# Centred rows, fp16 latents and a residual in the accumulator banks in a three-stage transformer layer

## The reference

```
x = x + xattn(layernorm(x), ctx[4096 x 512], mask)    # 16 heads of 32, output bias, layer norm of the scaled result
x = x + latent_attention(layernorm(x))                # 16 heads, causal
x = x + experts(layernorm(x))                         # top 8 of 48 kept experts, capacity 192
```

```
cq    = rms_norm(h @ w_qa.T, q_a_ln_w)                # 384 latents for each token
q     = cq @ w_qb.T                                   # for each head 128 plain and 64 rotary channels
ckv   = h @ w_kva.T                                   # 128 latents and 64 rotary key channels, the latter shared by all heads
k_pe  = k_pe * cos + rotate_half(k_pe) * sin
kv    = rms_norm(ckv[..., :128], kv_a_ln_w) @ w_kvb.T
out   = softmax(q k^T * scale, causal) v, @ w_o.T
```

## Time and profile before

| | us |
|---|---|
| median of 3 runs | 749.24 (747.83 to 749.28) |
| the profiled execution | 750.56 |
| its span, first to last instruction | 748.7 |
| TensorE busy | 719.0 |
| VectorE, ScalarE, GpSimd busy | 610.7, 428.7, 10.3 |

### The profile page before, as it was taken

One profiled execution on the slowest core, in us unless ns is written; L12 is line 12 of the kernel. 1 busy time (PEld: TensorE's weight loads), 2 busy tenths in 40 slices (PEclk: granted clock), 3 DMA queues, 4 the chain that ended last, 5 costly groups with the idle time before them and its releaser, 6 DMA issues.

```text
span 748.7 us, 16362 instructions
## 1 busy us (share of the span) xinstructions
PE 719.0 (96%) x6667; PEld 446.3 (60%) x6667; DVE 610.7 (82%) x940; ACT 428.7 (57%) x585; POOL 10.3 (1%) x30
## 2 busy tenths in 40 slices
PE   7999999999999999897999988999999999999997
PEld 3644444444444444455777757677777777777774
DVE  4578999999999988687788965788888888888885
ACT  3677777777777786623568733444444444444441
POOL 2000000000000000010000000000000000000000
PEclk9999999999999999999999999999999999999999
DMA  8920101010100100031242500497777777777760
GB/s 318 330 67 1 58 2 57 3 58 7 52 3 1 43 17 2 3 133 82 75 135 87 193 36 1 137 285 236 241 223 236 239 232 244 218 241 237 243 208 29
DMA packets 29576, 93.78 MB, mean 125 GB/s; under 512 B 5920, under 2 KB 15056, under 8 KB 28112
## 3 DMA queue, kind: packets, MB, share of 16 engines
q1 hardware_dynamic: 29232, 92.97, 37.8%
q10 hardware_dynamic: 288, 0.02, 0.0%
HBM read 92.37 MB, written 0.57 MB: 124 GB/s over the span
## 4 chain that ended last, share of the span: by engine, by line
PE 85%; DVE 6%; issue 4%; ACT 3%; POOL 1%; POOLq 0%; DVEq 0%; ACTq 0%
PE pS L1134 39%; PE pP L1134 26%; PE pO L1134 10%; PE pD L1134 8%; DVE x_sb L827 2%; ACT arena L508 2%; PE pO L1462 1%; DVE arena L714 0%; DVE bn L863 0%; DVE arena L842 0%; DVE arena L962 0%; DVE arena L914 0%; DVE xn L708 0%; ACT arena L558 0%; DVE work L868 0%
## 5 line engine op out<-in xcount | busy, mean ns | idle before, releaser
L1134 PE MATMUL pS<-arena 128*128 128x256 f16 (+2 forms) x2128 | 252.6, 275 | 5.1 <-DVE arena L962 1.3
L1134 PE MATMUL pP<-arena 128*128 128x512 f16 x968 | 236.4, 383 | 7.0 <-DVE arena L714 7.0
L1134 PEld LDWEIGHTS pS<-arena 128*128 128x128 f16 (+2 forms) x2128 | 212.0, 101 | 50.0 <-ACT arena L575 2.2
L1134 PEld LDWEIGHTS pP<-arena 128*128 128x128 f16 x968 | 90.9, 99 | 131.6 <-issue 11.7
L508 ACT ACTIVATE arena<-pS,mblk 128x1024 f32<-128x1024 f32 x128 | 147.3, 1205 | 11.5 <-PE pS L1134 11.5
L962 DVE SCALAR_TENSOR_TENSOR arena<-arena 128x1536 f16<-128x1536 f32 x72 | 126.0, 1752 | 0.6 <-ACT arena L613 0.5
L651 ACT ACTIVATE arena<-pS 128x256 f32<-128x256 f32 x72 | 27.6, 383 | 155.9 <-PE pS L1134 155.9
L815 DVE TENSOR_SCALAR arena<-arena 128x1024 f32<-128x1024 f32 x128 | 87.2, 690 | 26.2 <-ACT arena L508 23.1
L613 ACT ACTIVATE arena<-arena 128x1536 f16<-128x1536 f32 x72 | 106.3, 1477 | 1.0 <-DMA arena<-in_units 1.0
L1134 PE MATMUL pO<-arena 128*32 128x256 f32 (+6 forms) x1358 | 104.4, 359 | 2.4 <-DVE arena L952 1.9
L1134 PE MATMUL pD<-arena 128*128 128x512 f16 x288 | 76.5, 379 | 1.0 <-DVE arena L1106 1.0
(11 more groups left out here) (242 smaller groups left out, 504.7 us busy)
## 6 DMA issues: line engine op xcount, KB each, us to landing
arena<-in_units SPq DMA_DIRECT2D x72, 768.0 KB, 4.7
arena<-w_scratch SPq DMA_DIRECT2D x136, 64.0 KB, 2.7
arena<-in_ctxT SPq DMA_DIRECT2D x7, 1024.0 KB, 5.1
mw_in<-in_mla_in SPq DMA_DIRECT2D x8, 832.0 KB, 6.7
mw_out<-in_mla_out SPq DMA_DIRECT2D x8, 512.0 KB, 3.7
wlatT<-in_wlatT SPq DMA_DIRECT2D x1, 1280.0 KB, 11.4
arena<-in_wkT SPq DMA_DIRECT2D x4, 256.0 KB, 4.4
arena<-in_ctxT SPq DMA_DIRECT2D x4, 256.0 KB, 6.3
```

The source lines that it names most:

```text
L1134: return pe.matmul(o, lhsT, rhs, start=start, stop=stop, **kw)
```

## The change

1. Output bias of the cross-attention: ScalarE and VectorE make two fp16 halves of it, in rows 0 and 32 of `bo16`, and `out_rows` starts each bank with a product of `onerow` and `bo16`. VectorE takes statistics and centres straight from the bank.
2. Rows: VectorE's last step of `x1_sb` also gives the row sum; `xn` is `x1_sb` less its mean. Column sums, `center`, `scale_kpe` go. The variance comes from a square with row sum on ScalarE.
3. Latents: the weights are split in the last context block (`wlh`, `wll`); transposed rows are split too (`xh`, `xl`); products in fp16 in three parts. The latents' norm weights come as a row and are applied while scaling.
4. Keys are rotated in token rows (`rotate_keys`, table `cs_r`) ahead of their transposition, then split.
5. Latents are transposed and split by tile; the first head pair is projected by token halves (`first_proj`).
6. `prep_experts` moves into the last head pair. The cast of its output weights moves ahead of the exps on ScalarE. Unit 3 is split by ScalarE at the end of the last pair, by VectorE ahead of the copy of `wT`.
7. Residual: `residual(t)` adds `x1_sb`, times 4096, to `pD` and `pP` with an fp32 product in the last pair. Statistics and `xn` are taken from the banks, which stay open through the experts; both `add_zero` there go.
8. `lo_x(1)` goes ahead of `top_of(0)`; `gate_up(1)` is done in two halves around the transposition of the weights; in the last turn `gate_up(71)` goes ahead of `down(69)`. The two output tiles are scaled out by VectorE and ScalarE and stored by a DMA each.

```diff
+                    if last and i < HC:
+                        if i == 0:
+                            act.wait_ge(s["const_ready"], 1)
+                            act.wait_ge(s["row_in"], 64)
+                            act.activation(bo16[0:1, :], bo_b[0:1, :], ACT.Copy, scale=SW)
+                            act.activation(bo_t[32:33, :], bo_b[32:33, :], ACT.Copy, scale=SW).then_inc(s["bo_hi"], 1)
+                            act.wait_ge(s["lat_in"], 16)
+                        act.activation(wlh[:, i], wlatT[:, i], ACT.Copy, scale=SW).then_inc(s["wl_hi"], 1)
...
-                link(dve.tensor_tensor(work[:, t, :], d_ps[t], bo_b[:, :], ALU.add))
-                half_stats(work, t)
+                link(dve.bn_stats(bn[:, t, :], d_ps[t]))
+                link(dve.bn_aggr(mv[:, t, :], bn[:, t, :]))
...
+                link(dve.scalar_tensor_tensor(x1_sb[:, t, :], work[:, t, :], rstd[:, t:t + 1], x_sb[:, t, :],
+                                              ALU.mult, ALU.add, accum_out=xsum[:, t:t + 1]))
+                link(dve.tensor_scalar(xmean[:, t:t + 1], xsum[:, t:t + 1], 1.0 / HID, None, ALU.mult))
+                dve.tensor_scalar(xn[:, t, :], x1_sb[:, t, :], xmean[:, t:t + 1], None, ALU.subtract).then_inc(s["xn_ready"], 1)
...
-            rope_k_products()
-            lo_latents()
-            rope_k()
-            lo_k(0, 0, 1)
-            rope_mul(0, 0, 3)
+            lo_rows(0)
+            row_vars(0)
+            lo_rows(1)
+            rotate_keys(0)
+            row_vars(1)
+            add_eps(0)
+            norm_latents(0)
+            rotate_keys(1)
+            add_eps(1)
+            lo_latents(0)
+            norm_latents(1)
+            dve.wait_ge(s["kpe_hi"], 1)
+            dve.scalar_tensor_tensor(kpel, kpeT, SH / (SX * SW), kpeh, ALU.mult, ALU.subtract).then_inc(s["kpe_ready"], 1)
+            lo_latents(1)
...
+            def latents(t, low):
+                if low:
+                    pe.wait_ge(s["xl1_ready"], t + 1)
+                else:
+                    pe.wait_ge(s["xT_ready"], t + 2)
+                for o, lo, hi, done in ((kpe_ps[t], LAT, LAT + 2 * DR, "kpe_mm"), (lat_raw[t], 0, LAT, "lat_mm")):
+                    for c in range(HC):
+                        for x, w in (((xl, wlh),) if low else ((xh, wlh), (xh, wll))):
+                            last = mm(o, x[:, c, 128 * t:128 * t + 128], w[:, c, lo:hi], not low and c == 0 and w is wlh,
+                                      low and c == HC - 1)
+                    if low:
+                        last.then_inc(s[done], 1)
...
+            first_proj(0)
+            turn_latents(1)
+            first_proj(1)
             pe.wait_ge(s["kpe_ready"], 1)
             add_zero((pD[:, :], pP[:, :]), True, False)
             mla_pair(0, 0, before=False)
...
                 mla_scores(m, p, apart=True)
                 out_product(m - 1, 1 - p, 0)
+                residual(0)
                 turned(0)
+                residual(1)
                 weighted(0)
...
             lo_x(0)
+            lo_x(1)
             top_of(0)
             choose(0)
-            lo_x(1)
...
             last.then_inc(s["w_ready"], 1)
+            split_unit(AHEAD, AHEAD)
             dve.wait_ge(s["wt_done"], 1)
             dve.tensor_copy(wT, wt_ps).then_inc(s["wt_ready"], 1)
...
-                    if not (last_turn and u + 1 >= UNROLL) and not (first and u < 2):
+                    if not (last_turn and u + 2 >= UNROLL) and not (first and u < 2):
                         gate_up(n + 1, (u + 1) % 3, (u + 1) % RING)
-                    down(n, u % RING, u % 3)
+                    if last_turn and u + 3 == UNROLL:
+                        gate_up(n + 2, (u + 2) % 3, (u + 2) % RING)
+                    down(n, u % RING, u % 3, last_turn and u + 1 == UNROLL)
```

More of the change, by code:

```diff
@@ L33 @@
 SA, SW, SH = 64.0, 256.0, 16.0
+SX = 16.0
 NEG = -1.0e30
@@ L233, in build @@
         wnew = take(T)
+        lnw_b = take(LAT)
+        cs_r = take(TT * 2 * DR).rearrange("p (t i d) -> p t i d", t=TT, i=2)
+        bo16, bo_t = (take(HID, f16) for _ in range(2))
+        onerow = sb("onerow", [128, 128], f16)
         assert x_end <= ARENA
@@ L836, in x_block @@
                         (prep_scales, prep_rows)[i]()
+                    if last and i in (2, 3):
+                        for c in (2 * i - 4, 2 * i - 3):
+                            dve.wait_ge(s["wl_hi"], c + 1)
+                            dve.scalar_tensor_tensor(wll[:, c], wlatT[:, c], SW, wlh[:, c], ALU.mult, ALU.subtract)\
+                               .then_inc(s["wl_lo"], 1)
                     if last and i in (4, 6):
@@ L907, in add_eps @@
+                link(last)
+                for i, op in ((0, ALU.subtract), (1, ALU.add)):
+                    last = dve.tensor_tensor(kpn[:, t, i], kcos[:, t, i].unsqueeze(1).broadcast_to([128, 2, DR]),
+                                             ksin[:, t, 1 - i].unsqueeze(1).broadcast_to([128, 2, DR]), op)
+                last.then_inc(s["kpn_ready"], 1)
             def add_eps(t):
@@ L1372, in proj_q @@
+            def proj_q(m):
+                pe.wait_ge(s["qkv_ready"], 3 * m)
+                pe.wait_ge(s["qk_lo"], 2 * m)
+                pe.wait_ge(s["rope_ready"], m)
                 pe.wait_ge(s["mq_lo"], m + 1)
-                for r in ((1, 0) if first else (0, 1)):
-                    if r and not first and not (isinstance(m, int) and m == 1):
+                for r in range(2):
+                    if r and not (isinstance(m, int) and m == 1):
                         pe.wait_ge(s["a_lo"], m - 1)
@@ L1526, in _, with gate_up @@
                 last.then_inc(s["logits_done"], 1)
-            add_zero((pD[:, :], pP[:, :]), True, False).then_inc(s["down_done"], 1)
-            def gate_up(n, bank, ring):
+            def gate_up(n, bank, ring, halves=(0, 1)):
                 pe.wait_ge(s["unit_lo"], n + 1)
-                for half in range(2):
+                for half in halves:
                     k = 0
@@ L1539, in gate_up, with down @@
                             k += 1
-                last.then_inc(s["gu_done"], 1)
-            def down(n, ring, buf):
+                if 1 in halves:
+                    last.then_inc(s["gu_done"], 1)
+            def down(n, ring, buf, end=False):
                 pe.wait_ge(s["h_lo"], n + 1)
                 for t, o in enumerate((pD, pP)):
-                    for h, w in ((hh, uwh), (hh, uwl), (hl, uwh)):
-                        last = mm(o[:, :], h[:, buf, 128 * t:128 * t + 128], w[:, ring, HC * 256:UW], False, False,
+                    for k, (h, w) in enumerate(((hh, uwh), (hh, uwl), (hl, uwh))):
+                        last = mm(o[:, :], h[:, buf, 128 * t:128 * t + 128], w[:, ring, HC * 256:UW], False, end and k == 2,
                                   skip_group_check=True)
-                last.then_inc(s["down_done"], 1)
+                    if end:
+                        last.then_inc(s["moe_done"], 1)
+                if not end:
+                    last.then_inc(s["down_done"], 1)
             pe.wait_ge(s["xl_ready"], TT)
```

304 lines of the change are left out of this document (156 added, 148 removed).

## The result

The changed kernel takes 737.83 us, the median of 4 runs (737.12 to 738.79); the kernel before took 749.26 beside it (747.83 to 749.96). The ratio is 0.985, with a 95% interval of 0.983 to 0.987: 11.4 us faster. The profiled execution took 737.29 us, span 735.6, against 750.56 and 748.7 before, so the spans differ by 13.1 us.

The account below looks back on a forecast made before the run. TensorE, busy 719.0 of 748.7 us, was taken as the bound, with gains only in three seams where it waits. Terms summed to -12.85 us, giving 737.7 (profiled) or 736.4 (median); forecast 737.0, range 734.3 to 741.2.

Parts of the forecast that it names:

- Part 1: Last context block, ahead of the first seam: added ScalarE casts cost 0.6 us, two output-bias products 0.4; together +1.0 us.
- Part 2: First seam, first output product to first latent-attention scores: 23.0 us instead of 26.9, so -3.9 us.
- Rival (b): First seam doesn't shorten: thirteen hand-overs each 0.3 us late use up the 3.9 us; total 740.3 us, chance 0.17.
- Part 3: First scores of the latent attention: 36 score matmuls at full clock take 2.20 us instead of 3.37; -1.1 us.
- Part 4: Last head pair and way into the experts: fourth unit starts at 465.0 instead of 471.1 us; -6.1 us.
- Part 5: The end: no wait before the last down products, no zero products, two engines empty banks, half stored early; -2.75 us.
- (a): Clock falls in the latents instead, doubling fp16 products' time, some 1.2 us reaching the chain; total 738.7 us, chance 0.17.
- (c): TensorE falls to half clock at the last pair's end and stays down into the experts; five such units give 755.9; chance 0.03.
- (d): Attention's buffers shift in SBUF, costing 1.7 us in each of seven pairs; total 748.3 us, chance 0.03.

## Why the prediction was right

The forecast was 737.0 us, the range 734.3 to 741.2; it came out at 737.83. Step by step:

- **Part 1, +1.0: +1.1, by other shares.** ScalarE's first turn lost 0.87, not 0.6. Its timeline has the three casts one behind the other and the next exp after them; the one-row casts take as long as the row said, but I had let them start 0.5 us apart, and they go at 0.62 and 0.66:

```profile
296.39 0.61 ACT L549 ACTIVATE arena<-bo_b 1x512 f16<-1x512 f32 x1
297.01 0.63 ACT L550 ACTIVATE arena<-bo_b 1x512 f16<-1x512 f32 x1
297.67 0.74 ACT L552 ACTIVATE arena<-wlatT 128x640 f16<-128x640 f32 x1
298.31 1.19 ACT L534 ACTIVATE arena<-pS,mblk 128x1024 f32<-128x1024 f32 x1
```

  The bias products cost 0.12 and 0.13 us of the chain instead of 0.22 each. The version with the casts in another block got back 0.87. Two errors that nearly cancel, so that the sum came out at +1.1 is in part luck.
- **Part 2, 23.0 us: 22.94.** The points on the way hold too: rows ready at 3.4 (3.3), products from 4.9 (4.7), tile 1's products done at 12.0 (12.0), tile 0's latents at 12.4 (12.5), first half projected from 14.6 (14.6), second half's low part at 18.7 (19.0), first scores at 22.9 (23.0). The row sum costs one instruction of 0.08 us a tile, inside the 0 to 0.2. Two experiments show what binds it: 1.08 us a tile less for TensorE brought nothing, 2.19 us more for VectorE cost 1.70. That doesn't make TensorE's work there free: the eight products that took 3.51 us for 1.89 at the half clock moved the first scores by 1.69. The two paths are close, since TensorE's transposes of tile 1 start at 335.70 and their rows are ready at 335.3. Rival (b) wanted hand-overs 0.3 us late each; between engines they are 0.02 to 0.14 in the chain. Its argument against, "5.4 us of fp32 products go", counts one tile: both tiles' fp16 products take 6.6 of the 8.67 us by the prediction's own sum.
- **Part 3, -1.1: -1.0, and less sure than it looks.** The scores took 2.37 us for 3.37, at full clock in this execution. Filling that one gap in the kernel before moved the fall, in the profiled execution, instead of removing it.
- **Part 4, -6.1: -6.1.** The first product ends 2.36 us sooner (2.4, although the terms written out for it, 0.57, 1.23 and 0.46, give 2.26), the rows are ready 3.5 sooner (3.3), although taking one out of its bank cost 0.80 us and not 0.69:

```profile
L1088 DVE TENSOR_SCALAR xn<-pP,mv,rstd 128x512 f32<-128x512 f32 x1 | 0.8, 809 | 0.0
```

  The Trainium skill, "VectorE: DVE Perf Modes", section "Why PSUM operands drop a tier", spoke against the edit; this row bears it out more strongly than the rows of before did, and the edit still pays since two additions of 0.69 us went. The wait for the experts' preparation was 0.17 us (0.3). The clock's 1.69 and the split's 1.33 + 0.15 were tried alone: 1.68 and 1.24. The residual products cost nothing. They fill the gaps, but that they hold the clock up isn't shown: without them it stayed at 1.00 in the last pair as well.
- **Part 5, -2.75: -2.7.** The last down products follow without a wait, the copies run on two engines, the second half leaves at 732.99 and the span ends 2.6 us later. The order alone was given 1.1, which its row doesn't show (the timeline of the kernel before has 0.96 of idle time there), and measured 0.9.
- **The rivals.** (a) is partly true. The clock does fall in the latents in some executions, which the prediction named as a sign of being wrong ("a clock of 0.50 in a seam"). Of 16 executions of the four kernels whose code is the same up to the last pair, ten had a mean clock of 0.997 or 0.998; two of the four profiled ones show the fall, at 334 to 338 us, and it cost 1.69 us up to the first scores. The rival's size came out by two errors that nearly cancel: I let 1.2 us reach the chain, and gave back 1.1 at the scores, which in those two executions ran at full clock as well (2.37 us). The changed kernel's two executions at 0.997 and 0.998 took 738.36 and 738.79 us, where the rival's sum said 738.7; that their falls are in the latents isn't shown, as their traces weren't kept. I gave it 0.17 as if it held for all executions or none; it holds for half of them or more, and that puts the median between the two kinds, 0.8 us above the forecast. (c) and (d) didn't come: clock 1.00 from the last pair on, steady unit and steady pairs as before.
- **The median moved 11.4 us and the spans 13.1.** Of 33 executions of the kernel before beside the experiments, five had a mean clock of 1.000, and took 746.96 to 747.65 us; 19 had 0.995, and took 748.69 to 750.16. At full clock in both, the change is 747.0 to 737.2: 9.8 us. The profiled one of before had both falls (2.86 us by the earlier trace rows), that of after none. So about 10 us of the gain are work and order, and the rest is that the falls became rarer (28 of 33 executions below 1.000 before, 10 of the 16 above after the change). I had put 2.8 of the sum down to the clock; the profile alone can't tell how often a fall comes, the list of executions can.

## What to carry to other kernels

In a seam between two dense stages, write out the chain of hand-overs to the instruction, with each engine's queue in order: the step that stands ahead of yours in its queue (a preparation on VectorE, the turn behind a projection on TensorE) can cost nearly its full length (1.70 of 2.19 us here). Taking work from TensorE in between may bring nothing, and the same work at the half clock may still cost all that it grows by (1.69 us). Work for a later stage that fits into a TensorE wait (the residual as a product, half a unit early) was free here and makes the sparse stretch denser. Look at the mean granted clock of every execution before comparing medians: where falls to half clock come in some executions only, filling one gap may move them, and filling all of them took away the slow executions here (of five for each of two kernels) and didn't shorten the others.

## What the runs showed of the hardware

- A fall to the half clock isn't fixed to a gap. The changed kernel and the one without the residual run the same code in the latents, behind the same waits of TensorE (1.76 and 0.78 us): one ran its eight products at 1.00 in 1.89 us, the other had 0.53 in that window and took 3.51. With the same waits of 0.87 and 1.08 us in the first pair, one kernel ran on at 1.00 and another at 0.50; the kernel with less TensorE work ahead had the lower mean clock in all four executions (0.995). What decides between them stays open; no run here separates it. The Trainium skill, "TensorE: Matmul & The Clock Gate", section "What's actually happening", says that the number of matmuls at the half clock is not the same from run to run of one kernel, and ties that to the kernel's start; the executions here show the like for falls in its middle: of 33 of the kernel before, five had a mean clock of 1.000.
- Two more fp16 products of 512 columns in front of fp32 ones cost 0.12 and 0.13 us and not 0.22 each. TensorE's timeline has the bias product overlapping the fp32 one behind it, whose weights then load under it:

```profile
324.15 0.39 PE L1170 MATMUL pP<-arena,onerow 128*128 128x512 f16 x1
324.38 1.88 PE L1170 MATMUL pP<-arena 128*128 128x512 f32 x4
```

  That the weight load is the reason is an inference from the timeline of the weight loads, which has two of the fp32 products' from 324.15, and was not tried alone.
- A VectorE instruction that also gives a row sum adds an instruction of its own, 0.08 us, behind the main one:

```profile
L916 DVE DVE_READ_ACCUMULATOR x_sb<-work,rstd,x_sb 128x1 f32 x2 | 0.2, 80 | 0.0
```

- An fp32 tensor-scalar of 512 columns with two per-row scalars took 0.80 us out of a bank, 0.54 us out of SBUF.
